# Mixture-of-experts results added to the output in DRAM by accumulating scatters, instead of read back and summed per tile of tokens

## The chip, the cores and the metric

The kernel runs on one core of a Trainium2 chip. The metric is device time in microseconds (us), the median of several executions. One execution of the kernel before was also recorded by the hardware profiler; all rows below are from it.

## The reference

One transformer block with modulation from a conditioning vector, all in float32:

```
x = L0_attn_x                                  # (4, 1024, 256)
sa, ca, ga, sb, cb, gb = silu(c) @ wmod        # per batch; |ga|, |gb| held above 0.25
h = layernorm(x) * (1 + ca) + sa
x = x + ga * attention(h)                      # 16 heads of 16, causal, with output projection
h = layernorm(x) * (1 + cb) + sb
x = x + gb * moe(h)
```

`moe(h)`: logits of 8 experts for each of the 4096 tokens, the two largest chosen, their softmax as weights; each expert is `silu(h @ w1[e]) @ w2[e]` with a hidden width of 512; a token's result is the weighted sum over its two experts. The reference computes all experts for all tokens; the kernel computes only the chosen pairs of token and expert.

## The kernel before

Attention runs first, batch by batch, in 16 groups of four heads. `schedule()` writes one list of steps, in order, for the whole kernel; each engine walks through it and issues its own part of each step, so the list sets the order on every engine and on both DMA-issuing queues (SP's and POOL's). Semaphore waits are between steps.

After attention of a batch, step `x2` stores the residual stream x of that batch to DRAM (tensor X2), steps `h2` normalise and modulate it in place, and `h2st` stores that to DRAM (H2D, rows of 256 numbers). Routing gives each of the 8192 pairs a place in a list sorted by expert, padded to whole tiles of 128 rows: NF = 71 tiles. Segment 0 (batches 0 to 2) fills tiles 0 to 40, segment 1 (batch 3, and what is left over) tiles 41 to 70. Steps `hot`, `tok` and `table` turn this round into three tables: TOK (the token's row for each row of a tile), ROW (where its result goes) and TE (the tile's expert).

Then 71 tiles go through the experts. In iteration t of the loop (line 281) the order is: `xload` t+3, `ystore` t-3, `up` t, `turnx` t+1, `turnh` t-1, `down` t-2.
- `xload` (L906, POOL queue): a gather by TOK of 128 rows of H2D into XL, three buffers; it waits for the transposes of tile t-3.
- `turnx` (L1666, L1667, L1031, L1443): TensorE transposes XL; ScalarE and VectorE split the result in a high and a low part.
- `up` (L1481, PH): 6 matrix products with the expert's w1; ScalarE applies SiLU (L1037). `turnh` (L1688, L1045, L1448): transposes and the same split.
- `down` (L1481, PY): 12 products with w2; VectorE copies PSUM to YO (L1455), four buffers.
- `ystore` (L912, POOL queue): a scatter by ROW of YO into the DRAM tensor YT, in which each token has a row for its first and one for its second expert. No two scatters write the same row, and none waits for another.

The last attention steps of batch 3 (`div`, `out`, `ln2`, `logits`, routing of segment 1) are interleaved with the first 40 tiles or so.

At the end each of the 32 tiles of 128 tokens is combined. `gat` (L785, L787, SP queue) loads its rows of X2 into XR and its two rows per token of YT into YG, after the scatters of all tiles that can hold them. `comb` weights the first result (L1051, ScalarE), adds the weighted second (L1460), multiplies by gb (L1464) and adds x (L1467, all VectorE). `out_st` (L792) stores the tile. The 24 tiles of segment 0's batches run beside experts' tiles 56 to 70; the 8 of batch 3 wait for the last scatter.

Of the kernel before, what the change touches and what calls it, by code (L numbers as in the profile page):

```python
# [17 lines left out]
NG = 4 * B  # L18
# [19 lines left out]
EMPTY = 128 * (NF - NA)  # L38

# [49 lines left out]
def schedule():  # L89
# [37 lines left out]

    def table(s, at, rest, late):
# [8 lines left out]
    def combine(n):  # L137
        return [(0, ("comb", n)), (0.5, ("out_st", n))]
# [43 lines left out]
    place(1, 12, one("gates"))  # L182
    place(0, -36, one("bvb"))
# [13 lines left out]
    place(NG - 1, 16, one("weights", 0))  # L197
# [83 lines left out]
    for t in range(NF + 12 + NT):  # L281
# [16 lines left out]
        while at and min(at) <= (t if t < NF + 11 + NT else max(at)):  # L298
# [14 lines left out]

LATE = ()

RING = 10


def gat_ring(n):

    return n % RING if n < 3 * NT else RING + n - 3 * NT
# [43 lines left out]
    "weights": {"wt": 3},  # L367
    "hot": {"hot": 1},
    "tok": {"px": 1, "tok": 1},
    "table": {"table": lambda s, n: 2 + s * (2, 1, 0, 0, 0)[n]},  # L370
# [6 lines left out]
    "xload": {"xl0": lambda t: 16 * (t % 3 == 0), "xl1": lambda t: 16 * (t % 3 == 1), "xl2": lambda t: 16 * (t % 3 == 2)},  # L377
    "turnx": {"fx": 1, "xhi": 1, "xlo": 1},
# [4 lines left out]
    "gat": {f"yg{i}": (lambda n, i=i: 32 * (gat_ring(n) == i)) for i in range(RING + NT)},  # L383
    "comb": {"cmb_a": 1, "comb": 2, "cmb_d": lambda n: int(n not in LATE), "cmb_p": lambda n: int(n in LATE)},
    "out_st": {f"o{i}": (lambda n, i=i: 16 * (gat_ring(n) == i)) for i in range(RING + NT)},
}

FIRST = {"c0": 16, "gbb": 16 * B, "wm0": 16, "wm1": 16, "ld_xa": 16, "ld_x0": 16, "ld_x1": 16, "ld_x2": 16, "ld_x3": 16, "ld_w": 16, "ld_bq": 16, "ld_o": 48, "ld_gw": 16,
# [30 lines left out]
def adaln_block(nc, x, wqkvT, b_qk, b_v, woT, b_o, gate_w, w1, w2, cT, wmod, iota, out):  # L419
# [8 lines left out]
    with ctx:  # L428
# [12 lines left out]
        TW = sb("TW", [128, 2, B * NT])  # L441
# [11 lines left out]
        TM1 = sb("TM1", [128, 2, NF])  # L453
        DU = sb("DU", [128, NF - NA])
# [70 lines left out]
        XL = sb("XL", [128, 3, D], F32, ffn)  # L525
        GB = sb("GB", [128, B, D], F32, ffn)
        end = ExitStack()
        YG = [sb(f"YG{i}", [128, 2, D], F32, end) for i in range(4)]
        XR = [sb(f"XR{i}", [128, D], F32, end) for i in range(4)]

        G3R = G3[:, :, :, :].rearrange("p b t n -> p (b t) n")
        YG += [XB[:, 3 * i:3 * i + 2, :] for i in range(2)] + [G3R[:, 3 * i:3 * i + 2, :] for i in range(4)]
        XR += [XB[:, 3 * i + 2, :] for i in range(2)] + [G3R[:, 3 * i + 2, :] for i in range(4)]
        end.close()
# [4 lines left out]

        last = ExitStack()  # L540
        YG += [sb(f"YGL{i}", [128, 2, D], F32, last) for i in range(NT)]
        XR += [sb(f"XRL{i}", [128, D], F32, last) for i in range(NT)]
        last.close()

# [19 lines left out]
        X2 = nc.dram_tensor("X2", [B, T, D], F32).ap()  # L564
        H2D = nc.dram_tensor("H2D", [B * T, D], F32).ap()

        YT = nc.dram_tensor("YT", [EMPTY + B * T * 2, D], F32).ap()
# [65 lines left out]
        def x2_tiles(b):  # L633
            return X2[b].rearrange("(t p) d -> p t d", p=128)

        def store_wait(lane, tiles):

            for t in range(tiles - 4, tiles):
                lane.wait_ge(*after(f"ys{t % 4}", "ystore", t))
# [4 lines left out]
        def sync_program(eng):  # L644
# [16 lines left out]
            for step in order:  # L661
# [75 lines left out]
                elif kind == "x2":  # L737
                    b = a[0]
                    sp.wait_ge(*after("om", "out", b, 3))
                    eng.dma_start(x2_tiles(b), xt(b * NT, (b + 1) * NT)).then_inc(S[f"x2{b}"].sem, 16)  # L740
                elif kind == "h2st":
# [3 lines left out]
                    eng.dma_start(H2D[b * T:(b + 1) * T, :].rearrange("(t p) d -> p t d", p=128),  # L745
# [22 lines left out]
                elif kind == "gat":  # L768
                    n = a[0]
                    b, r = n // NT, gat_ring(n)  # L770
                    if n == 0:
                        sp.wait_ge(*after("om", "out", B - 1, 3))
                        sp.wait_ge(*after("px", "tok", 1, 0))
                        for i in range(B):
                            eng.dma_start(GB[:, i, :].rearrange("p (k n) -> p k n", k=2),
                                          GD.rearrange("(t k b) n -> b t k n", k=2, b=B)[i, 3].partition_broadcast(128)
                                          ).then_inc(S["gbb"].sem, 16)
                        sp.wait_ge(S[f"h2s{B - 1}"], 16)
                        sp.wait_ge(*after("px", "lgt", B - 1, 3))
# [973 lines left out]
```

## Time and profile before

| | us |
|---|---|
| median of 3 runs | 1033.56 (1031.01 to 1035.2) |
| the profiled execution's own time | 1026.26 |
| its span | 1024.5 |
| TensorE busy | 910.5 (89% of the span) |
| VectorE busy | 738.2 (72%) |
| ScalarE busy | 577.4 (56%) |
| GpSimd busy (mostly issuing indirect DMAs in the last third) | 347.4 (34%) |

PE is TensorE's matmuls, PEld its weight loads, DVE VectorE, ACT ScalarE, POOL GpSimd, SP SyncE, which only issues DMAs. "L912" is line 912 of the kernel. A row of the timeline gives start and duration in us, engine, line, operation, and in brackets how long the engine had been idle and what ended that. The chain of waits is followed back from the last instruction of the execution.

### The profile page before, as it was taken

The numbers are of one execution on the slowest core, as the hardware profiler recorded it, in microseconds if no ns is written. First come the engines' busy times: TensorE is split into PE (matmuls) and PEld (weight loads), VectorE is DVE, ScalarE is ACT, GpSimd is POOL, SyncE is SP. The second block draws the span as 40 slices with busy tenths as digits, with TensorE's granted clock in tenths as the row PEclk, the third lists the DMA queues.
The fourth block names the chain that finished last, engine by engine and source line by source line (L and its number), as shares of the span: only waits on it lengthen the run. The fifth ranks groups of instructions, "written<-read, shape, count | busy, mean of one in ns | idle before, by whom it ended". The sixth has DMA issues, their size and how long they took to land.

```text
span 1024.5 us, 19379 instructions
## 1 busy us (share of the span) xinstructions
PE 910.5 (89%) x6174; PEld 535.3 (52%) x6174; DVE 738.2 (72%) x2346; ACT 577.4 (56%) x1257; POOL 347.4 (34%) x302
## 2 busy tenths in 40 slices
PE   5798899998899999989999888878699999999990
PEld 3443335333445334544443443423498899999880
DVE  8788766879666889757689767799337675444697
ACT  3235576676586667576666747557534534334452
POOL 1422021242424124325003433003177456655630
PEclk8899899999999999999999997989999999999995
DMA  8436436327316166253463565103413323222698
GB/s 275 123 63 125 62 77 140 62 39 145 66 27 138 41 101 139 66 74 89 73 117 100 124 112 170 36 23 111 137 47 124 99 68 104 78 78 68 207 297 293
DMA packets 83235, 110.61 MB, mean 108 GB/s; under 512 B 15930, under 2 KB 56434, under 8 KB 83138
## 3 DMA queue, kind: packets, MB, share of 16 engines
q1 hardware_dynamic: 75506, 89.45, 37.4%
q0 software_dynamic: 6816, 18.62, 5.8%
q10 hardware_dynamic: 816, 1.32, 0.4%
q8 instruction: 53, 0.87, 0.4%
q14 instruction: 44, 0.36, 0.1%
HBM read 69.42 MB, written 35.41 MB: 102 GB/s over the span
## 4 chain that ended last, share of the span: by engine, by line
PE 63%; DVE 14%; ACT 11%; issue 5%; POOL 3%; DMA 3%; SPq 1%; POOLq 0%; ACTq 0%; DVEq 0%
PE PO L1604 11%; PE PY L1481 9%; PE PS L1584 9%; PE PH L1481 9%; PE PM L1561 8%; ACT PR L979 5%; PE PHT L1688 3%; PE PX L1616 2%; PE PX L1530 2%; DVE MXF L1282 2%; PE PS L1588 2%; PE PX L1633 2%; DVE JK L1279 2%; PE PX L1539 1%; PE PX L1540 1%
## 5 line engine op out<-in xcount | busy, mean ns | idle before, releaser
L979 ACT ACTIVATE PR<-PS 128x512 f32<-128x512 f32 (+3 forms) x768 | 335.1, 497 | 165.0 <-PE PS L1588 128.4
L1279 DVE CUSTOM_DVE_ANT_0 JK<-PM,MK 128x128 bf16<-128x128 f32 (+3 forms) x512 | 239.6, 484 | 57.8 <-PE PM L1561 56.9
L1561 PE MATMUL PM<-QK 128*128 128x512 bf16 (+3 forms) x768 | 251.5, 336 | 26.9 <-DVE MXF L1282 15.6
L1584 PE MATMUL PS<-QK 128*128 128x512 bf16 (+3 forms) x768 | 250.7, 337 | 12.5 <-ACT PR L979 10.3
L1282 DVE TENSOR_REDUCE MXF<-PM 128x1 f32<-128x512 f32 x256 | 175.2, 684 | 76.5 <-PE PM L1561 74.8
L1584 PEld LDWEIGHTS PS<-QK 128*128 128x128 bf16 x768 | 75.2, 98 | 175.3 <-ACT PR L979 110.1
L1604 PE MATMUL PO<-PR,V 128*17 128x512 f32 (+3 forms) x1536 | 164.0, 500 | 0.0
L1561 PEld LDWEIGHTS PM<-QK 128*128 128x128 bf16 x768 | 76.0, 99 | 101.0 <-DVE MXF L1282 36.3
L1481 PE MATMUL PY<-W2S,HT 128*128 x852 | 120.2, 291 | 4.9 <-issue 4.3
L1037 ACT ACTIVATE HS<-PH 128x512 f32<-128x512 f32 x71 | 42.5, 598 | 135.4 <-PE PH L1481 133.3
L906 POOL DMA_INDIRECT XL<-H2D,TOK x71 | 78.7, 1109 | 113.6 <-DVE TE L1422 65.1
L1481 PE MATMUL PH<-W1S,XT 128*128 x426 | 112.5, 399 | 4.0 <-DVE XT L1443 3.5
L1588 PE MATMUL PS<-MT,identb 128*128 128x128 bf16 x512 | 112.5, 222 | 0.0
L1481 PEld LDWEIGHTS PY<-W2S,HT 128*128 128x128 f32 x852 | 107.2, 191 | 5.6 <-issue 5.5
L1443 DVE TENSOR_TENSOR XT<-PXT,XT 128x256 fp32r<-128x256 f32 x71 | 30.0, 422 | 106.6 <-ACT XT L1031 106.6
L847 POOL TENSOR_TENSOR SF<-SF,SP 128x512 f32<-128x512 f32 x28 | 32.4, 1157 | 215.2 <-ACT SP L969 215.1
L912 POOL DMA_INDIRECT YT<-YO,ROW x71 | 74.9, 1055 | 85.2 <-DVE YO L1455 76.1
L1481 PEld LDWEIGHTS PH<-W1S,XT 128*128 128x128 f32 x426 | 75.7, 189 | 18.3 <-issue 5.9
L1588 PEld LDWEIGHTS PS<-MT,identb 128*128 128x128 bf16 x512 | 50.8, 99 | 33.0 <-issue 6.3
L865 POOL TENSOR_TENSOR OP<-OP,LP 128x1024 f32<-128x1024 f32 x7 | 16.5, 2357 | 125.5 <-DMA LP<-LR 125.5
L1448 DVE TENSOR_TENSOR HT<-PHT,HT 128x512 fp32r<-128x512 f32 x71 | 49.0, 690 | 4.0
L1604 PEld LDWEIGHTS PO<-PR,V 128*17 128x17 f32 x1536 | 25.6, 96 | 34.4 <-issue 25.9
(263 smaller groups left out, 1201.6 us busy)
## 6 DMA issues: line engine op xcount, KB each, us to landing
QK<-SD SPq DMA_DIRECT2D x180, 128.0 KB
SD<-SP SPq DMA_DIRECT2D x42, 256.0 KB, 2.7
OP<-OS SPq DMA_DIRECT2D x64, 64.0 KB
LP<-LR SPq DMA_DIRECT2D x64, 64.0 KB, 2.3
W1S<-in_w SPq DMA_DIRECT2D x8, 512.0 KB, 5.8
W2S<-in_w SPq DMA_DIRECT2D x8, 512.0 KB, 4.8
X<-XA SPq DMA_DIRECT2D x3, 1024.0 KB, 9.1
H2D<-XA SPq DMA_DIRECT2D x3, 1024.0 KB, 4.9
```

Source lines behind the costliest of these rows:

```text
L906: eng.indirect_dma_start(XL[:, t % 3, :], None, H2D[0:(B if t >= NA else B - 1) * T, :], bass.IndirectOffsetOnAxis(ap=TOK[:, t:t + 1], axi ...
L912: eng.indirect_dma_start(YT, bass.IndirectOffsetOnAxis(ap=ROW[:, t:t + 1], axis=0), YO[:, t % 4, :], None, bounds_check=EMPTY - 1 + B * T ...
L979: eng.activation(PR[:, slot, i, c0:512], PS[m % 3][:, c0:512], ACT.Exp, scale=0.25).then_inc(S["exp"].sem, 1)
L1037: eng.activation(HS[:, t % 2, :], PH[t % 2][:, :], ACT.Silu).then_inc(S["silu"].sem, 1)
L1279: eng.tensor_tensor_reduce(JK[:, jk % 2, 0:w], PM[m % 3][:, 0:w], MK[:, 512 - w:512], 1.0, -3.0e38, ALU.add, ALU.max, MXA[:, mb, h, qt:qt ...
L1282: eng.tensor_reduce(MXF[:, mb, h, qt - 4:qt - 3], PM[m % 3][:, 0:w], AX.X, ALU.max).then_inc(S["mx"].sem, 1)
L1448: eng.tensor_tensor(HT[:, t % 2, 1, :, :], PHT[t % 2][:, :, :], HT[:, t % 2, 0, :, :].bitcast(F32), ALU.subtract).then_inc(S["hlo"].sem, 1)
L1481: last = eng.matmul(out_, stat[:, part, c, :], wt[:, bass.ds(v, 1), c, :].rearrange("p a n -> p (a n)"), start=(j == 0 and c == 0), stop=( ...
L1561: eng.matmul(PM[m % 3][:, 0:128 * (k1 - k0)], QK[:, r, h, 0, qt * 128:(qt + 1) * 128], QK[:, r, h, 1, k0 * 128:k1 * 128], start=True, stop ...
L1584: last = eng.matmul(PS[m % 3][:, c0:512], QK[:, r, h, 1, j * 128:(j + 1) * 128], QK[:, r, h, 0, 512 * f + c0:512 * f + 512], start=True, s ...
L1588: last = eng.matmul(PS[m % 3][:, c0:c0 + 128], identb[:, :], MT[:, :], start=False, stop=True, skip_group_check=True)
L1604: last = eng.matmul(PO[32 * i:32 * i + 17, c0:512], V[g // 4 % 2][:, j, 4 * (g % 4) + i, :], PR[:, (m - 1 + i // 2) % SLOTS, i % 2, c0:512 ...
```

## The change

- The output tensor in DRAM becomes 4096 + 128 rows; the first 4096 are returned. Step `x2` stores the residual x straight into its rows. The last 128 are filled once (with rows of x) and take the results of padding rows.
- `ystore` becomes an accumulating scatter (`compute_op=ALU.add`) to the token's row of the output. Since a token has two experts, a row can be hit by two tiles, so `ystore` t now waits until `ystore` t-1 has landed.
- The factors must be in the tile before it is stored. H2D's rows grow to 514 numbers: h, the row of gb of the token's batch (written by step `grow`, four DMAs on ACT's queue, DRAM to DRAM), and the token's two weights (step `wst`, SP queue, in pieces of 8 bytes). `xload` gathers all 514. A new DVE instruction in `turnx` picks the weight of this row's expert (WP), and the copy PSUM to YO becomes one instruction that multiplies by it and by gb.
- XL becomes a ring of six buffers that are held until YO is made: `xload` t waits for `down` t-6, not for the transposes of t-3.
- `gat`, `comb`, `out_st`, YT, X2 and the loads of gb (GB) are gone; the loop ends three iterations after the last tile.
- The tables are computed a little differently: ROW is the token, KK selects the weight.

```diff
-    place(45, one("weights", 1))
-    for n in range(3 * NT):
-        place(NL + 2.5 + 0.6 * n, one("gat", n))
-        place(NL + 4.5 + 0.6 * n, combine(n))
-    for n in range(3 * NT, B * NT):
-        place(NF + 2, one("gat", n))
-        place(NF + 8 + n - 3 * NT, combine(n))
+    place(24, weights(1))
...
-    for t in range(NF + 12 + NT):
+    for t in range(NF + 3):
...
+                elif kind == "wst":
+                    s = a[0]
+                    sl = slice(SEGS[s][0] * NT, SEGS[s][1] * NT)
+                    sp.wait_ge(*after("wt", "weights", s))
+                    eng.dma_start(H2D[:, 2 * D:WIDE].rearrange("(n p) k -> p n k", p=128)[:, sl, :],
+                                  TW[:, sl, :]).then_inc(S["ws"].sem, 16)
+            for i in range(4):
+                sp.wait_ge(S[f"ys{i}"], S[f"ys{i}"].n)
...
                 elif kind == "xload":
                     t = a[0]
-                    po.wait_ge(*after("table", "table", int(t >= NA), 4))
-                    for b in range(B if t >= NA else B - 1):
+                    s = segment(t)
+                    rows = SEGS[s][1] * T
+                    po.wait_ge(*after("table", "table", s, 4))
+                    for b in range(SEGS[s][1]):
                         po.wait_ge(S[f"h2s{b}"], 16)
-                    if t >= 3:
-                        po.wait_ge(*after("fx", "turnx", t - 3))
+                    po.wait_ge(S["gr"], 16 * B)
+                    po.wait_ge(*after("ws", "wst", s))
+                    if t >= XS:
+                        po.wait_ge(*after("yo", "down", t - XS))
...
                 elif kind == "ystore":
                     t = a[0]
+                    s = segment(t)
+                    rows = B * T + 128 if s else SEGS[0][1] * T
                     po.wait_ge(*after("yo", "down", t))
+                    for b in range(SEGS[s][1]):
+                        po.wait_ge(S[f"x2{b}"], 16)
+                    if s:
+                        po.wait_ge(S["dz"], 16)
+                    if t:
+                        po.wait_ge(*after(f"ys{(t - 1) % 4}", "ystore", t - 1))
                     eng.indirect_dma_start(
-                        YT, bass.IndirectOffsetOnAxis(ap=ROW[:, t:t + 1], axis=0), YO[:, t % 4, :], None,
-                        bounds_check=EMPTY - 1 + B * T * 2, oob_is_err=True).then_inc(S[f"ys{t % 4}"].sem, 16)
+                        out[0:rows, :], bass.IndirectOffsetOnAxis(ap=ROW[:, t:t + 1], axis=0), YO[:, t % 4, :], None,
+                        bounds_check=rows - 1, oob_is_err=True, compute_op=ALU.add).then_inc(S[f"ys{t % 4}"].sem, 16)
...
+                elif kind == "grow":
+                    b = a[0]
+                    ac.wait_ge(*after("gd", "gates"))
+                    eng.dma_start(H2D[b * T:(b + 1) * T, D:2 * D].rearrange("r (k n) -> r k n", k=2),
+                                  GD.rearrange("(t k b) n -> b t k n", k=2, b=B)[b, 3].partition_broadcast(T)
+                                  ).then_inc(S["gr"].sem, 16)
...
                 elif kind == "turnx":
                     t = a[0]
+                    dv.wait_ge(*after("table", "table", segment(t), 4))
+                    dv.wait_ge(*after(f"xl{t % XS}", "xload", t))
+                    if t >= XS:
+                        dv.wait_ge(*after("yo", "down", t - XS))
+                    eng.tensor_tensor_reduce(WJ[:, t % XS, :], XLS[t % XS][:, 2 * D:WIDE], KK[:, t, :], 1.0, 0.0, ALU.mult, ALU.add,
+                                             WP[:, t % XS:t % XS + 1]).then_inc(S["wp"].sem, 1)
...
                     if t >= 4:
                         dv.wait_ge(*after(f"ys{t % 4}", "ystore", t - 4))
-                    eng.tensor_copy(YO[:, t % 4, :], PY[t % 2][:, 0:256]).then_inc(S["yo"].sem, 1)
+                    dv.wait_ge(*after("wp", "turnx", t))
+                    eng.scalar_tensor_tensor(out=YO[:, t % 4, :], in0=PY[t % 2][:, 0:D], scalar=WP[:, t % XS:t % XS + 1],
+                                             in1=XLS[t % XS][:, D:2 * D], op0=ALU.mult, op1=ALU.mult).then_inc(S["yo"].sem, 1)
```

## Rows read from the trace of the kernel before

**Rows 1.** The page: span, and the chain of waits by engine.
```profile
span 1024.5 us, 19379 instructions
PE 63%; DVE 14%; ACT 11%; issue 5%; POOL 3%; DMA 3%; SPq 1%; POOLq 0%; ACTq 0%; DVEq 0%
```

**Rows 2.** Windows: start:end, length, busy us of each engine, PEclk, DMA share, GB/s.
```profile
741.00:820.00 79.00, 76.49 (x531) 69.15 (x531) 43.57 (x128) 36.05 (x73) 51.98 (x46) 1.00 0.28 88
823.00:945.00 122.00, 122.00 (x857) 111.14 (x856) 65.70 (x165) 47.75 (x105) 71.64 (x68) 1.00 0.26 81
985.00:1000.00 15.00, 14.01 (x97) 12.30 (x95) 13.93 (x34) 7.69 (x17) 4.93 (x5) 1.00 0.91 290
```

**Rows 3.** Timeline: first YO, tile 19's and 20's, the last three.
```profile
740.53 0.43 DVE L1455 COPY YO<-PY 128x256 f32<-128x256 f32 x1 [3.14 <-PE PY L1481]
...
822.74 0.42 DVE L1455 COPY YO<-PY 128x256 f32<-128x256 f32 x1
823.98 1.03 POOL L912 DMA_INDIRECT YT<-YO,ROW  x1 [1.33 <-DVE YO L1455]
825.31 1.04 POOL L906 DMA_INDIRECT XL<-H2D,TOK  x1 [0.30 <-issue]
826.22 0.42 DVE L1455 COPY YO<-PY 128x256 f32<-128x256 f32 x1
827.45 1.03 POOL L912 DMA_INDIRECT YT<-YO,ROW  x1 [1.10 <-DVE YO L1455]
...
995.52 0.41 DVE L1455 COPY YO<-PY 128x256 f32<-128x256 f32 x1
...
997.77 0.42 DVE L1455 COPY YO<-PY 128x256 f32<-128x256 f32 x1
...
1000.72 0.42 DVE L1455 COPY YO<-PY 128x256 f32<-128x256 f32 x1
```

**Rows 4.** The scatter's line L912, issue to landing, 900 to 950 us.
```profile
L912 POOL DMA_INDIRECT YT<-YO,ROW x14: 1029/1031/1039, 900.9 to 947.9; - x14
DMA to landing us min/median/max: 2.5/2.5/2.5
```

**Rows 5.** The same line, 985 to 1004 us, beside the loads of the combine.
```profile
L912 POOL DMA_INDIRECT YT<-YO,ROW x6: 982/983/996, 985.9 to 1001.9; - x6
DMA to landing us min/median/max: 3.6/4.4/5.2
```

**Rows 6.** Chain of waits, order of time, after the last tile: start, us, what.
```profile
1000.72 0.43 DVE YO L1455
...
1001.20 0.49 issue
1001.70 0.22 POOLq L428
1001.92 4.54 DMA YT<-YO,ROW
...
1006.55 4.55 DMA YGL<-YT
...
1011.13 0.52 ACT YGL L1051
...
1021.84 0.42 DVE XRL L1467
```

**Rows 7.** DMA view, 823 to 945 us: POOL's queue, packets, MB, share of 16 engines.
```profile
q0 software_dynamic: 3312, 9.05, 23.4%
XL<-H2D,TOK POOLq DMA_INDIRECT x34
YT<-YO,ROW POOLq DMA_INDIRECT x34, 2.5
```

**Rows 8.** DMA view, whole span: queue, count, KB each, us to landing.
```profile
LP<-LR SPq DMA_DIRECT2D x64, 64.0 KB, 2.3
LP<-LD SPq DMA_DIRECT2D x8, 32.0 KB, 1.7
LR<-LP SPq DMA_DIRECT2D x8, 32.0 KB, 1.5
X<-XA SPq DMA_DIRECT2D x3, 1024.0 KB, 9.1
```

**Rows 9.** Timeline of DVE, one tile's interval beside two combines.
```profile
965.70 0.42 DVE L1455 COPY YO<-PY 128x256 f32<-128x256 f32 x1
966.04 0.48 DVE L1460 SCALAR_TENSOR_TENSOR YG<-YG,TW 128x256 f32<-128x256 f32 x1
966.55 0.43 DVE L1464 TENSOR_TENSOR YG<-YG,GB 128x256 f32<-128x256 f32 x1
...
969.60 0.41 DVE L1455 COPY YO<-PY 128x256 f32<-128x256 f32 x1
```

**Rows 10.** ACT's queue: one DMA issue, ns min/median/max.
```profile
L926 ACTq DMA_DIRECT2D W<-in_wqkvT x1: 521/521/521, 1.9 to 1.9; - x1
```

**Rows 11.** Windows around the loads of the next group's QK.
```profile
268.00:286.00 18.00, 15.98 (x122) 9.98 (x120) 8.70 (x28) 12.09 (x28) 9.68 (x8) 1.00 0.68 100
286.00:300.00 14.00, 13.22 (x82) 5.50 (x81) 9.31 (x29) 12.01 (x26) 1.16 (x1) 1.00 0.05 9
```

More of the change, by code:

```diff
@@ L126, in route, with weights @@
         return [(0 if n % many else rest, ("route", s, n)) for n in range(NR)]
+    def weights(s):
+        return [(0, ("weights", s)), (0, ("wst", s))]
     def table(s, at, rest, late):
@@ L182, in schedule @@
     place(1, 12, one("gates"))
+    for b in range(B):
+        place(3 + b, 2, one("grow", b))
     place(0, -36, one("bvb"))
@@ L196, in schedule @@
     place(NG - 2, 0, route(0, 0.5))
-    place(NG - 1, 16, one("weights", 0))
+    place(NG - 2, 6, weights(0))
     for k, parts in table(0, 6, 0.5, 2):
@@ L297, in schedule @@
             order.append(("down", t - 2))
-        while at and min(at) <= (t if t < NF + 11 + NT else max(at)):
+        while at and min(at) <= (t if t < NF + 2 else max(at)):
             now[0] = min(at)
@@ L367 @@
     "weights": {"wt": 3},
+    "wst": {"ws": 16},
+    "grow": {"gr": 16},
     "hot": {"hot": 1},
     "tok": {"px": 1, "tok": 1},
-    "table": {"table": lambda s, n: 2 + s * (2, 1, 0, 0, 0)[n]},
+    "table": {"table": lambda s, n: (2 + 2 * s, 2 + s, 2, 2, 3)[n]},
     "h2st": {f"h2s{i}": (lambda b, i=i: 16 * (b == i)) for i in range(B)},
@@ L376 @@
     "low": {"sp_d": lambda e: 1 + int(e == 2)},
-    "xload": {"xl0": lambda t: 16 * (t % 3 == 0), "xl1": lambda t: 16 * (t % 3 == 1), "xl2": lambda t: 16 * (t % 3 == 2)},
-    "turnx": {"fx": 1, "xhi": 1, "xlo": 1},
+    "xload": {f"xl{i}": (lambda t, i=i: 16 * (t % XS == i)) for i in range(XS)},
+    "turnx": {"fx": 1, "wp": 1, "xhi": 1, "xlo": 1},
     "up": {"fh": 1, "silu": 1},
@@ L524, in adaln_block @@
         sb("PAD1", [128, D], F32, ffn)
-        XL = sb("XL", [128, 3, D], F32, ffn)
-        GB = sb("GB", [128, B, D], F32, ffn)
+        XL = sb("XL", [128, 2, WIDE], F32, ffn)
+        XLS = [XL[:, i, :] for i in range(2)]
+        G3R = G3[:, :, :, :].rearrange("p b t n -> p (b t n)")
+        XLS += [G3R[:, WIDE * i:WIDE * (i + 1)] for i in range(XS - 2)]
         end = ExitStack()
[L528 to L534, printed above, removed]
         HOTS.append([sb("OLO1", [128, 1, PAIRS[1], 128], BF16, end), sb("OHI1", [128, 1, PAIRS[1], NF - NA], BF16, end),
@@ L538, in adaln_block @@
         ffn.close()
[L540 to L543, printed above, removed]
         PX = ps("PX", [128, 512])
@@ L633, in x2_tiles, with segment @@
         def x2_tiles(b):
[L634 to L639, printed above, removed]
+            return out[b * T:(b + 1) * T, :].rearrange("(t p) d -> p t d", p=128)
+        def segment(t):
+            return int(t >= NA)
         def od_wait(lane, g):
@@ L794, in sync_program @@
-            for i in range(RING + NT):
-                sp.wait_ge(S[f"o{i}"], S[f"o{i}"].n)
+                elif kind == "wst":
[6 more added lines that the diff above has]
+                sp.wait_ge(S[f"ys{i}"], S[f"ys{i}"].n)
@@ L1660, in tensor_program @@
                     t = a[0]
-                    pe.wait_ge(*after(f"xl{t % 3}", "xload", t))
+                    pe.wait_ge(*after(f"xl{t % XS}", "xload", t))
                     if t >= 1:
```

144 lines of the change are left out of this document (43 added, 101 removed).

## The prediction, made before the changed kernel was run

> **What bounds the kernel now.** I read the page first [rows 1]: TensorE carries 63% of the chain that ended last, DMA only 3%. The change touches the last third, so the next view is the windows over the experts' tiles. From 823 to 945 us TensorE is busy for 122.00 of 122 us at a granted clock of 1.00, while VectorE has 65.70 and POOL 71.64 [rows 2]. There nothing but TensorE sets the pace, and the period is the distance of two copies to YO: 826.22 - 822.74 = 3.48 us; over many tiles 3.47, which I use [rows 3]. Between 741 and 820 us steps of batch 3's attention take TensorE too and tiles come every 5.2 us at times: from the first copy (740.53) to tile 19's (822.74) 19 periods take 82.2 us, 4.33 each [rows 3]. From tile 19 to tile 70 (1000.72) 51 periods take 178.0 us, 3.49 each. Last, the chain of waits behind the last tile [rows 6]: copy at 1000.72, scatter issued at 1001.92, landed after 4.54 us, then a load of 4.55 us, then ScalarE and eight combines on VectorE up to 1022.3, then the last store up to the end at 1024.5. That is 1024.5 - 1001.1 = 23.4 us without any matmul. This tail is what the change can win; the scatters themselves are hidden now, since none waits for another.
>
> **What the change removes.** In the tail only the last scatter is left. It was slow (4.54 us; 3.6 to 5.2 beside the loads of the combine, DMA share 0.91) [rows 2, 5, 6]; in quiet stretches it takes 2.5 from issue to landing [rows 4]. With 0.78 us from the end of the copy (1001.14) to the start of POOL's instruction (1001.92) [rows 3, 6], the tail shrinks to 0.8 + 2.5 = 3.3 us if the add costs nothing: 20.1 won. The combines that run beside tiles 56 to 70 go as well. One interval with two of them on VectorE is 969.60 - 965.70 = 3.90 instead of 3.47 [rows 9]; five intervals in that stretch are so, 5 x 0.43 = 2.2 us. But the last two tiles come 2.3 and 3.0 us after the ones before them (995.52, 997.77, 1000.72) [rows 3], closer than scatters in line can follow (below), which takes about 1.5 back. Sum of what can be won: 20.1 + 2.2 - 1.5 = about 21 us.
>
> **What it adds: scatters in line.** `ystore` t waits for the landing of `ystore` t-1. POOL needs 0.78 us from a release to the start of an indirect DMA (823.16, the end of the copy, to 823.98 is 0.82; the last is 0.78) [rows 3, 6], and that counts in each link, because the wait is the last to end. So scatters can't follow each other faster than P = L + 0.78, with L from issue to landing. For the plain scatter P = 2.5 + 0.78 = 3.28 us [rows 4], against 3.47 that TensorE gives: the chain is hidden, by 0.19 us. So the whole forecast hangs on what the add does to L. Queued behind the waiting instruction on POOL is the gather `xload` of t+4; when it is held, XL comes late, TensorE waits, and the tiles take P as well; the four YO buffers only soften that.
>
> Below what L is this free? Up to P = 3.47 (L = 2.69) nothing is lost. Above that I follow it: with the chain the bound, slack in the slow first 19 tiles absorbs it (4.33 mean against P), and tile 19's scatter starts at 823.16 + 0.78 + 1.04 + 0.30 = 825.3, behind the gather that is now released by the same copy [rows 3]. Then 51 links and one landing: end of span = 825.3 + 51 x (L + 0.78) + L = 865.1 + 52 L. It equals 1024.5 at L = 3.07. Half a microsecond in L decides the sign, and each 0.1 us above costs 5.2 us (more beyond P = 4.33, where the first tiles are held too: by a small recurrence over all 71 copies, +57 us at L = 4.0).
>
> The trace shows no accumulating DMA, so L is bounded. Below: 2.5, the plain scatter [rows 4]. It can't be shorter, as the same bytes are still sent to the same kind of place. Above: the add as a load of its own ahead of the write; the nearest load is LP<-LR, 64 KB, 2.3 us [rows 8], so 4.8. Between them: a scatter's or gather's share of the 16 DMA engines is 0.234 x 122 / 68 = 0.42 us [rows 7]; the add must read 128 KB more, so its data part about doubles: +0.42. A read of DRAM must come back before the write: a 32 KB load takes 1.7 against 1.5 for a store of the same size [rows 8]: +0.2. POOL's 1.03 us [rows 4] is descriptor writing for 128 rows; a third address for each row would be up to half more, +0.5, or nothing if that time is fixed: I take +0.2. L = 2.5 + 0.42 + 0.2 + 0.2 = 3.3 us, P = 4.1, both nearer to the plain scatter's row than to the other bound. End of span 865.1 + 52 x 3.3 = 1036.7: +12.2 us.
>
> The Trainium skill, "Collectives: The Full Stack", section "The bandwidth ceiling: the fold count and why AG ≠ RS ≠ AR", says that the add in the DMA engine costs no cycles of its own, and that it is the second read that halves the rate. By that rule only the doubled data part counts, L = 2.9, and the span would end at 1015.9, 8.6 us early; no row here shows an add, so the trace neither bears it out nor speaks against it. It is the third case below. Its page "DMA: Bandwidth & Descriptors", section "Rules for kernel authors", adds that another write to the same bytes that lands during an accumulate is lost, so the wait between scatters can't be left out here.
>
> **Other edits.** The copy to YO becomes a multiply with a second operand: 0.48 instead of 0.42 [rows 9], and a small instruction on 2 columns is added, at most 0.2. VectorE then has some 0.3 us more per tile at 65.70/122 = 54% busy [rows 2]: hidden by TensorE; if that cover went it would be 71 x 0.3 = 21 us. The gather carries 257 KB instead of 128 and is released 2 us later, but TensorE wants it two periods later, 6.9 us, and by the scatter's row and the doubled data it lands in 2.5 + 0.42, some 3 us: nothing. The four `grow` DMAs are issued by ScalarE during attention, 0.52 us each [rows 10], and carry 4 MB from DRAM to DRAM. They fall on the loads of the next group's QK, when the DMA engines are full for 14 us (share 0.68 over 18 us, then 0.05) [rows 11]; a store of 1 MB lands in 9.1 [rows 8], so these loads could end 9 us late where they have about 10 to spare. I take +1 us for the four, bounds 0 and +8. `wst` is off every path: segment 0's weights stand in the order a whole group of attention before the first gather, and segment 1's at iteration 24, fourteen before tile 41 is gathered. The tables have about as many small instructions as before, and lie beside a TensorE that is never idle there [rows 2]: 0. The store of x into the output has the bytes of the old one: 0.
>
> **Sum.** +12.2 + 1 = +13 us on the profiled execution's span; its own time goes from 1026.3 to 1039.5. The runs have a median of 1033.56, 7.3 above the profiled one; the same +13 gives 1047.
>
> **The cases.**
> - Chain of scatters is the bound, L of 3.1 or more (chance 0.6). For it: the margin of 0.19 us is smaller than any of the three additions. Own range: L from 3.1 to 4.0, +2 to +57: 1036 to 1091; value 1047.
> - The chain stays hidden, L up to about 2.75 (chance 0.15). For it: 16 engines hold eight rows each, and reads of one row may run beside writes of another, so that only a small part of the extra read shows. Then the tail's 21 us are won, less 1: 1014.
> - Chain longer than TensorE's period but shorter than break-even, L of 2.75 to 3.0, what the second read alone gives (chance 0.2). 865.1 + 52 x 2.9 = 1015.9, 8.6 early, less 1: 1026 on the runs.
> - The scatters are free, but QK's loads come late four times by `grow` (chance 0.05): 4 x 2 = +8 against -21: 1021. Against it: waits for QK's loads don't show in the chain now.
> The mechanism on the other side is thus one: whether L stays below 3.07 us.
>
> That the change doesn't do what it says can be ruled out for the tail: no step reads back.
>
> **Chances.** A difference of under 0.5% (5 us) is no change by what can be measured here. Faster by more: 0.33 (cases two and four and most of three); within: 0.09 (L of 2.97 to 3.17); slower: 0.58. The range of 8 in 10 goes from 1015, which leaves part of the hidden chain out, to 1088 (L = 4.0).
>
> **What would show it.** Right: L912 shows landings of 3.3 us and is released by its own DMA in most of its 71 instances, its starts 4.1 us apart after 823; TensorE busy some 85% of that stretch, PE PXT waiting for the gather; no matmul-free tail beyond the last scatters. Wrong: starts still 3.47 apart and TensorE at 100% (hidden, the tail won); or landings above 4.0 (then it costs 60 us and more); or idle before PM<-QK about groups 5 to 8.

## The result, and the profile after

| | us |
|---|---|
| changed kernel, median of 4 runs | 1136.46 (1130.28 to 1146.09) |
| before, on the same chip, median of 4 runs | 1034.38 (1031.01 to 1037.2) |
| ratio, with its 95% interval | 1.0997 [1.0912, 1.1082] |
| span of the profiled execution | 1135.7 (before 1024.5, [rows 1]) |

The change makes the kernel 10% slower. The forecast was +13 us, and the range ended at 1088: the direction was right, the size far off. The two profiled spans differ by 111.2 us, and the place of the first copy to YO splits them: 740.53 before [rows 3] and 785.95 now. So 45.4 us come before the first expert's tile is finished, and 65.8 us behind it.

The page of the kernel after: span, the chain of waits by engine, and the same chain by line.

```profile
span 1135.7 us, 19288 instructions
PE 35%; DMA 26%; DVE 10%; issue 9%; ACT 8%; SPq 6%; POOL 5%; POOLq 0%; another core or an unknown queue 0%; ACTq 0%; DVEq 0%
DMA out<-YO,ROW 20%; PE PO L1560 9%; PE PS L1540 7%; PE PM L1517 6%; SPq L658 4%; ACT PR L948 3%; PE PX L1486 2%; DVE MXF L1245 2%; DVE JK L1242 2%; PE PX L1572 2%; PE PS L1544 1%; DMA LD<-OS 1%; PE PX L1495 1%; PE PX L1496 1%; ACT SF L931 1%
```

TensorE carried 63% of the chain before [rows 1]; now it is 35%, and DMA went from 3 to 26, of which the accumulating scatter has 20. SPq, which is SP's queue itself, went from 1 to 6; 4 of these are L658, the loads of QK.

First the scatters. The scatter's line in the kernel after: durations in ns, min/median/max, and who releases it, in us and times.

```profile
L881 POOL DMA_INDIRECT out<-YO,ROW x71: 1552/1589/3625, 788.5 to 1129.3; - x71
its engine sat idle before it (us, times) until:
  DMA out<-YO,ROW: 85.8, 45
```

The same scatter in the DMA view: KB are not given, the last number is the median us from issue to landing.

```profile
out<-YO,ROW POOLq DMA_INDIRECT x71, 3.8
```

One such instruction on POOL takes 1.59 us where the plain scatter took 1.03, and it lands after 3.8 us where that one took 2.5 [rows 4]. In 45 of 71 cases POOL sits idle until the scatter before has landed. The chain of waits at the end (start, us, what) shows the links themselves:

```profile
1110.65 3.84 DMA out<-YO,ROW
...
1115.33 3.82 DMA out<-YO,ROW
1119.14 0.02 issue
1119.16 0.02 POOLq L399
1119.18 0.04 issue
1119.23 0.03 POOLq L881
1119.26 0.72 issue
1119.98 3.84 DMA out<-YO,ROW
...
1124.65 3.78 DMA out<-YO,ROW
```

Landing at 1119.14, next start at 1119.98: 0.84 us. A link, from the start of one scatter to the start of the next, is 3.8 + 0.85 = 4.65 us, against the 3.47 us in which TensorE makes a tile. What TensorE makes of it is in the windows (start:end, length, busy us of each engine, PEclk, DMA share, GB/s):

```profile
823.00:945.00 122.00, 99.48 (x683) 86.58 (x684) 70.80 (x255) 46.49 (x90) 68.36 (x50) 0.99 0.50 97
```

It was busy for all of these 122 us before [rows 2]; now for 99.48. It waits for gathers, as the waits of 740 to 1136 us say (engine and line, what it waited for: us in total, times, longest). The ring of six buffers appears there under two names, XL and G:

```profile
PE PXT L1622 <- DMA G<-H2D,TOK: 36.1, 29, 3.1
PE PXT L1622 <- DMA XL<-H2D,TOK: 16.3, 13, 2.8
```

The gathers are late because they stand on POOL behind a scatter that waits for its predecessor.

The tail that the change was to win is nearly as long as before: 21.1 us from the last copy to YO (1114.57) to the end, against 23.8. The copies run ahead of the chain, and the scatters left over follow one another there.

Now the part ahead of 786 us. `grow` in the DMA view, with its landing time, and SP's queue in the timeline (start, us, what):

```profile
H2D<-GD ACTq DMA_DIRECT2D x4, 1024.0 KB, 23.4
```

```profile
197.82 23.25 SPq L658 DMA_DIRECT2D QK<-SD  x12
```

Twelve issues of loads of QK took SP's queue 23.25 us, beside a `grow` issued at 200 us. The twelve issues at the same place in the kernel before:

```profile
197.78 6.15 SPq L685 DMA_DIRECT2D QK<-SD  x12
```

Twelve take 25.51 and 17.30 us beside the second and the fourth `grow`. The third was issued at 311.14, when the loads of its group were already out (302.00 to 307.57); beside it four other loads take 13.80. Each group of attention begins its loads with one QK<-ZR, and the distances between these show what each `grow` cost. Before they start at 196.97, 234.11, 272.27, 317.26 and 354.74, now at 197.00, 246.48, 301.19, 347.74 and 399.54: 12.3, 16.6, 1.6 and 14.3 us more, 44.8 of the 45.4. The one `grow` that met no load of QK cost next to nothing.

In the windows from 200 to 420 us (columns as above), first after, then before, TensorE loses 34 us and its granted clock is 0.90 instead of 1.00:

```profile
200.00:420.00 220.00, 171.08 (x1113) 74.78 (x1135) 131.82 (x443) 120.16 (x267) 48.72 (x39) 0.90 0.46 88
```

```profile
200.00:420.00 220.00, 205.33 (x1436) 92.78 (x1433) 174.01 (x620) 151.18 (x339) 67.01 (x54) 1.00 0.47 91
```

The DMA share is the same over these 220 us, 0.46 and 0.47, and nearly so the bytes, 88 and 91 GB/s. So a want of bandwidth doesn't explain it; `b_growx` below confirms this with engines that are fully busy.

### The profile page after: what moved, and what is told of

The parts are those of the page before. It is cut to its first block, busy times and chain, and to the rows that moved or that the text cites. A ratio compares the mean times of both kernels' runs of the same rounds, so it can differ in the third digit from the quotient of the medians.

```text
span 1135.7 us, 19288 instructions
## 1 busy us (share of the span) xinstructions
PE 925.3 (81%) x6098; PEld 538.4 (47%) x6174; DVE 715.3 (63%) x2394; ACT 572.9 (50%) x1225; POOL 389.0 (34%) x302
## 4 chain that ended last, share of the span: by engine, by line
PE 35%; DMA 26%; DVE 10%; issue 9%; ACT 8%; SPq 6%; POOL 5%; POOLq 0%; another core or an unknown queue 0%; ACTq 0%; DVEq 0%
DMA out<-YO,ROW 20%; PE PO L1560 9%; PE PS L1540 7%; PE PM L1517 6%; SPq L658 4%; ACT PR L948 3%; PE PX L1486 2%; DVE MXF L1245 2%; DVE JK L1242 2%; PE PX L1572 2%; PE PS L1544 1%; DMA LD<-OS 1%; PE PX L1495 1%; PE PX L1496 1%; ACT SF L931 1%
## 5 line engine op out<-in xcount | busy, mean ns | idle before, releaser
L1517 PE MATMUL PM<-QK 128*128 128x512 bf16 (+3 forms) x727 | 238.7, 336 | 62.3 <-DVE MXF L1245 42.5
L1540 PE MATMUL PS<-QK 128*128 128x512 bf16 (+3 forms) x733 | 240.5, 339 | 15.5 <-ACT PR L948 11.1
L1560 PE MATMUL PO<-PR,V 128*17 128x512 f32 (+3 forms) x1536 | 168.8, 513 | 0.1
L881 POOL DMA_INDIRECT out<-YO,ROW x71 | 115.4, 1625 | 125.3 <-DMA out<-YO,ROW 85.8
L866 POOL DMA_INDIRECT XL<-H2D,TOK x24 | 26.6, 1109 | 105.1 <-DVE ROW L1380 67.8
L866 POOL DMA_INDIRECT G<-H2D,TOK x47 | 53.3, 1134 | 13.7 <-issue 13.6
## 6 DMA issues: line engine op xcount, KB each, us to landing
H2D<-GD ACTq DMA_DIRECT2D x4, 1024.0 KB, 23.4
```

The lines of the kernel that those rows point to most:

```text
L866: eng.indirect_dma_start(XLS[t % XS], None, H2D[0:rows, :], bass.IndirectOffsetOnAxis(ap=TOK[:, t:t + 1], axis=0), bounds_check=rows - 1, ...
L881: eng.indirect_dma_start(out[0:rows, :], bass.IndirectOffsetOnAxis(ap=ROW[:, t:t + 1], axis=0), YO[:, t % 4, :], None, bounds_check=rows - ...
L1517: eng.matmul(PM[m % 3][:, 0:128 * (k1 - k0)], QK[:, r, h, 0, qt * 128:(qt + 1) * 128], QK[:, r, h, 1, k0 * 128:k1 * 128], start=True, stop ...
L1540: last = eng.matmul(PS[m % 3][:, c0:512], QK[:, r, h, 1, j * 128:(j + 1) * 128], QK[:, r, h, 0, 512 * f + c0:512 * f + 512], start=True, s ...
L1560: last = eng.matmul(PO[32 * i:32 * i + 17, c0:512], V[g // 4 % 2][:, j, 4 * (g % 4) + i, :], PR[:, (m - 1 + i // 2) % SLOTS, i % 2, c0:512 ...
```

## The experiments

Ratios are to the kernel before, run beside each on its chip. The first time given behind "Measured" is the median of the runs; positions ("first copy to YO") and spans are those of the profiled execution.

### Each half of the change alone, in the kernel before

`b_grow` adds only the four DMAs, into a scratch tensor that nobody reads:

```diff
+        place(3 + b, 2, one("grow", b))
...
+                    eng.dma_start(GROW[b * T:(b + 1) * T, D:2 * D].rearrange("r (k n) -> r k n", k=2),
+                                  GD.rearrange("(t k b) n -> b t k n", k=2, b=B)[b, 3].partition_broadcast(T)
```

> The kernel before, with nothing added but the four grow DMAs (4 MB, DRAM to DRAM, pieces of 512 bytes, on ACT's queue) into an unused DRAM tensor, at the same steps as in the changed kernel. Theory (grow alone delays attention by blocking the QK loads on SP's queue): first copy to YO near 786 us instead of 740.5, time near 1079 (+45). Rival (the delay of attention in the changed kernel comes of something else, or grow's 4 MB is hidden as predicted): within 8 us of before.

Measured: 1067.85 us, ratio 1.0391 [1.0322, 1.046], span 1067.6; first copy to YO at 783.66, 43.1 later than before. The DMAs land after 22.7 us. Nearly the whole early loss, 43.1 of 45.4 us, is there, with nothing else of the change.

`b_wait` adds only the wait from scatter to scatter, the scatters staying plain:

```diff
+                    if t:
+                        po.wait_ge(*after(f"ys{(t - 1) % 4}", "ystore", t - 1))
```

> The kernel before, with each plain scatter waiting for the landing of the one before it, and nothing else. Theory (a link costs L + 0.85 us, with L = 2.5 for the plain scatter it fits in the 3.47 us period): +0 to +6 us, all of it near the tail, where the scatter takes 3.5 to 4.4 us beside the combine's loads. Rival (waiting in line is itself the main cost, whatever the scatter does): +30 us or more.

Measured: 1043.58 us, ratio 1.015 [1.0099, 1.0202]: 15 us slower, more than the 0 to 6 expected, and far from the rival's 30. In the quiet stretch most links are 3.34 us, as forecast. Beside the loads of the combine (tiles 56 to 70), where landings took 3.6 to 5.2 us [rows 5], links are 3.3 to 6.6; the last copy to YO comes 11.8 us later than before. A chain has to be priced in its busiest stretch, not only in its quiet one. In the changed kernel these loads are gone.

### What in `grow` costs 45 us

`a_fix` is the changed kernel in which a `grow` loads the row once into all partitions of SBUF (128 KB) and stores from there, with pieces of 1 KB, at later steps of the group:

```diff
-                    eng.dma_start(H2D[b * T:(b + 1) * T, D:2 * D].rearrange("r (k n) -> r k n", k=2),
-                                  GD...[b, 3].partition_broadcast(T))
+                    eng.dma_start(GX.rearrange("p (k n) -> p k n", k=2), GD...[b, 3].partition_broadcast(128))
+                elif kind == "gput":
+                    eng.dma_start(H2D[b * T:(b + 1) * T, D:2 * D].rearrange("(t p) d -> p t d", p=128),
+                                  GX.unsqueeze(1).broadcast_to([128, NT, D]))
```

> The changed kernel, with grow sent another way: gb's row is first loaded to 128 partitions of SBUF (128 KB) and from there stored to H2D in pieces of 1 KB, at steps 12 and 15 of the same windows. Same result. Theory (form and place of grow cost 45 us): first copy to YO back near 741, time near 1090. Rival (any 4 MB more in attention costs that): stays above 1115.

Measured: 1089.09 us, ratio 1.0585 [1.0525, 1.0645]; first copy to YO at 736.17, links still 4.65. The early loss is gone and nothing else is: 61 us remain, and with the 40 of `b_grow` that makes 101, against the 102 of the change.

`a_late` leaves `grow` as it was and issues it seven positions later in the attention group:

```diff
-        place(3 + b, 2, one("grow", b))
+        place(3 + b, 9, one("grow", b))
```

> The changed kernel, with the four grow DMAs in their old form but at step 9 of the same windows instead of step 2, behind the QK loads instead of beside them. If the cost is the collision with the QK loads: near 1092, 45 us less than the changed kernel. If the 24 us that each DMA holds the DMA engines cost whatever comes: still above 1120. Between: other DMAs of the window (the rows of maxima, the stores of SD) wait behind it.

Measured: 1117.11 us, ratio 1.087 [1.0793, 1.0948]; first copy at 764.13, landing 20.9 us. By the profile the place halves the loss but doesn't remove it. Most of what stays comes from another load. The group with the second `grow` (issued at 243.16) takes 15.2 us more than before, and there a load of 32 KB, the sums of the softmax, lands late. It lands after 1.7 us in the kernel before [rows 8]. Its line from 240 to 260 us in `a_late`, who waited for it, and its landing:

```profile
L701 SPq DMA_DIRECT2D LP<-LD x1: 341/341/341, 247.9 to 247.9; - x1
  DVE LP L1277: 16.4, 1
DMA to landing us min/median/max: 16.8/16.8/16.8
```

`b_growx` takes `b_grow` and lets the DMAs, of the same size, at the same steps and from DRAM to DRAM, read a row of its own for each row that they write:

```diff
-                                  GD.rearrange("(t k b) n -> b t k n", k=2, b=B)[b, 3].partition_broadcast(T)
+                                  x[b].rearrange("r (k n) -> r k n", k=2)
```

> The kernel before plus four DMAs as in grow (1 MB each, DRAM to DRAM, pieces of 512 bytes, same steps, same queue), but with x's rows as the source, so that each piece is read from its own address instead of all 2048 from the same 1 KB. If the piece and the way (DRAM to DRAM) make the 23 us: landing near 23 us, time +40. If it is the re-reading of one row: landing below 12 us, time within 15 us of before.

Measured: 1024.98 us, ratio 0.9992 [0.996, 1.0023]; landing 9.4 us. The DMA view of `b_grow`, and then that of `b_growx`:

```profile
GROW<-GD ACTq DMA_DIRECT2D x4, 1024.0 KB, 22.7
```

```profile
GROW<-in_x ACTq DMA_DIRECT2D x4, 1024.0 KB, 9.4
```

Neither the 4 MB nor DRAM on both sides costs anything measurable. The windows of `b_growx` show the first of the four at work: the DMA engines are busy all the time, and TensorE hardly idles.

```profile
195.00:205.00 10.00, 9.72 (x81) 4.48 (x84) 8.65 (x30) 7.14 (x19) 0.00 (x0) 1.00 1.00 224
```

But the edit changed two things and not one. The queue of ACT on the pages of `b_grow` and of `b_growx`:

```profile
q10 hardware_dynamic: 9072, 5.51, 3.5%
```

```profile
q10 hardware_dynamic: 4976, 5.51, 2.0%
```

The same bytes take 4096 packets less. So the four DMAs moved in pieces of 512 bytes with gb's row as source, in pieces of 1 KB with x's rows, although the text above says 512 for both. Both the address that is read again and again and the number of pieces, 2048 against 1024 per DMA, can be the cause. The kernel before has DMAs that copy rows of GD into SBUF, in pieces of 512 bytes too:

```profile
G<-GD SPq DMA_DIRECT2D x4, 384.0 KB, 6.1
GB<-GD SPq DMA_DIRECT2D x4, 128.0 KB, 3.5
```

The four G<-GD, issued one behind the other from 141.4 us, write 3072 such pieces, each of twelve rows read 128 times, and land within 9 us. So neither pieces of 512 bytes nor 128 readings of a row are slow in themselves when they go to SBUF. What remains is one row read 2048 times, or 2048 small pieces from DRAM to DRAM, or both together; no run here separates them.

In `b_grow` TensorE waits 9.1 us for one load of QK between 200 and 420 us, and 28.2 us more are put down to VectorE's maxima (MXF); in `b_growx` no wait for QK shows there, and 4.5 us for MXF.

### What in the scatters costs 61 us

`a_fix_plain` is `a_fix` with plain scatters in the same chain, so the tokens' sums are left out:

```diff
-                        bounds_check=rows - 1, oob_is_err=True, compute_op=ALU.add)
+                        bounds_check=rows - 1, oob_is_err=True)
```

> The changed kernel with grow sent by way of SBUF, its scatters in line but plain: they overwrite the rows instead of adding, so sums are left out. Theory (the add makes L 3.8 instead of 2.5): landings 2.5, links 3.3 to 3.4, below the period of 3.47, span near 1007 plus what grow still costs, some 85 us below the same kernel with the add. Rival (waiting in line or the wider gather is the cost): span above 1060.

`a_fix_rows` is `a_fix` with accumulating scatters, but each to a block of 128 rows of its own, one of 16 blocks in turn, and without waits; the sums are left out too:

```diff
-                    if t:
-                        po.wait_ge(*after(f"ys{(t - 1) % 4}", "ystore", t - 1))
...
-                            eng.tensor_copy(ROW[:, ts], TK[:, 0, ts]).then_inc(tb.sem, 1)
+                            eng.scalar_tensor_tensor(out=ROW[:, t0:t1], in0=IO[:, 0:t1 - t0], scalar=128.0,
+                                                     in1=PI[:, 0:1].broadcast_to([128, t1 - t0]), op0=ALU.mult,
+                                                     op1=ALU.add).then_inc(tb.sem, 1)
```

> The changed kernel with grow by way of SBUF, accumulating scatters that wait for none: each tile adds to rows of its own among 16 places, in contiguous rows, so the tokens' sums are left out. Theory (the add only costs where the next scatter waits for it): tiles every 3.5 us, L912's successor still 1.6 us on POOL and landing in 3.8 or a little more, span near 1010. Rival (adds are slow in throughput: the DMA engines or POOL can't do one each 3.47 us): tiles above 4 us apart, span above 1050.

Measured: 1015.18 us, ratio 0.9821 [0.9715, 0.9927], and 1008.66 us, ratio 0.9758 [0.97, 0.9816]. The scatter's line from 880 to 980 us in `a_fix`, `a_fix_plain` and `a_fix_rows`, one fence each:

```profile
L884 POOL DMA_INDIRECT out<-YO,ROW x21: 1589/1589/1590, 882.9 to 975.9; - x21
  DMA out<-YO,ROW: 28.8, 17
DMA to landing us min/median/max: 3.7/3.8/3.9
```

```profile
L884 POOL DMA_INDIRECT out<-YO,ROW x28: 1029/1030/1042, 879.3 to 979.7; - x28
  DMA out<-YO,ROW: 6.2, 6
```

```profile
L882 POOL DMA_INDIRECT out<-YO,ROW x30: 1591/1591/1593, 879.0 to 979.7; - x30
```

In these 100 us the three kernels start 21, 28 and 30 scatters; the kernel before starts 29. The chain alone is hidden (links of 3.30 between slower ones), the add alone is hidden (1.59 us on POOL, tiles 3.47 apart for the most part). From first to last copy to YO the two take 261.9 and 262.4 us, the kernel before 260.2 and `a_fix` 329.9. Only both together cost: the add makes L 3.8, the chain puts all of L on the path. That `a_fix_rows` writes contiguous rows doesn't explain its speed: `z` below adds to the tokens' scattered rows without waits, its scatters land after 3.9 us in the median, and its tiles too come 3.47 apart up to the first sum. Between the chained add and the chained plain scatter lie 7.6% of the time, some 79 us, by the ratios (about 66 to 91 with their intervals; `a_fix_plain` has only two runs), and 70 us by the profiled spans, 1087.5 and 1017.5.

`a_fix_64` is `a_fix` with scatters of the tile's first 64 rows only; the others' results are left out:

```diff
-                        out[0:rows, :], bass.IndirectOffsetOnAxis(ap=ROW[:, t:t + 1], axis=0), YO[:, t % 4, :], None,
+                        out[0:rows, :], bass.IndirectOffsetOnAxis(ap=ROW[0:64, t:t + 1], axis=0), YO[0:64, t % 4, :], None,
```

> The changed kernel with grow by way of SBUF; each accumulating scatter stores only 64 of a tile's 128 rows, so half the results are left out. It divides the 1.3 us that the add puts on L into a part by rows and a fixed part. If POOL's 1.59 us is by rows: about 0.8 to 1.3, and landing 0.3 us less after it. If fixed: 1.59 and 3.8 stay. Expected from POOL by rows for the added part only (0.56 us): about 1.0 to 1.3 us on POOL, L near 3.1, span near 1040.

Measured: 1043.22 us, ratio 1.0096 [1.0064, 1.0129]. The same line and stretch:

```profile
L884 POOL DMA_INDIRECT out<-YO,ROW x25: 1439/1439/1457, 882.3 to 979.2; - x25
```

The time came out as expected (span 1039.2), the 1.0 to 1.3 us on POOL did not. Half the rows take only 0.15 us off POOL's 1.59. If that is linear, no more than 0.3 us of the 1.59 goes by rows, so of the 0.56 that the add puts on POOL at least 0.26 is fixed; how much more isn't shown, since no plain scatter of 64 rows was run. The link falls by 0.68 us, from 4.65 to 3.97, so 0.53 us of it lie outside POOL's instruction.

### Is there a version that wins?

The chain is there because two tiles can hit one row. `z` takes that reason away: based on `a_fix`, the second expert's results go to a second, zero-filled half of a larger output tensor, no scatter waits for another, and at the end of a batch one accumulating DMA of 1 MB adds the second half to the first. The padding rows go to four blocks in turn.

```diff
-                    if t:
-                        po.wait_ge(*after(f"ys{(t - 1) % 4}", "ystore", t - 1))
...
+                elif kind == "sum":
...
+                    first, second = [out[r:r + T, :].rearrange("(p t) d -> p (t d)", p=128) for r in (b * T, SECOND + b * T)]
+                    eng.dma_start(first, second, accum_op=ALU.add, max_dma_last_dim=8192)
```

> Full result, built from what the runs showed: grow by way of SBUF; accumulating scatters that wait for none, since a token's first result is added to its row of the output (which holds x) and its second to a row of a second half, filled with zeros during attention; tiles' padding rows go to four blocks in turn. After the last scatter one accumulating DMA per batch adds the second half to the output, 1 MB each, three of them beside the last tiles. Expected: tiles at 3.5 us as in the run without waits, last scatter near 1000 us, then 3.8 + 0.9 + a 1 MB accumulate of 5 to 9 us: span 1011 to 1016, about 13 us below before (ratio near 0.985). Rival: the accumulates of the first three batches, on POOL's queue, hold up its gathers, or the 4 MB of zeros delay attention: span above 1025.

Measured: 1026.75 us, ratio 0.9998 [0.9974, 1.0022], span 1020.6: no gain on the kernel before, a miss by some 5 us. The last copy to YO comes at 1004.64 where `a_fix_rows` had 997.93. A gather issued 1.8 us behind a sum (984.34 and 986.12) landed late, and TensorE waited; the gather's line from 980 to 1000 us in `z`:

```profile
L878 POOL DMA_INDIRECT G<-H2D,TOK x2: 1071/1104/1137, 981.9 to 986.1; - x2
  PE PXT L1666: 2.6, 1
DMA to landing us min/median/max: 4.5/6.9/9.2
```

`z2` was to cut the sums into pieces of 256 KB:

```diff
-        place(NL + 4 + 3 * b, one("sum", b))
+        for q in range(4):
+            place(NL + 4 + 8 * b + 2 * q, one("sum", b, q, 4))
```

> The version z with its sums in smaller pieces: each of the three early batches' sums is four DMAs of 256 KB, one every second tile from tile 45 on, where z issued 1 MB at once at three places; the last batch's sum is two DMAs of 512 KB where z had one. Theory (a gather queued behind a 1 MB accumulate lands late, 9.2 us in z, and holds TensorE): a gather now waits behind a quarter of it, so lands in at most 5 us, within the ring's slack; the last copy to YO comes at 998 to 1001 instead of 1004.6, and the span is 1013 to 1017 instead of 1020.6; on the runs 3 to 8 us faster than before. Rival (it is POOL's issuing time, or the DMA share as such, not the size of one transfer): twelve issues of about 1 us on POOL in place of three of 1.5 add work there and the bytes are the same, so the last copy stays at 1004 or later and the time stays equal to before's.

Measured: 1031.05 us, ratio 1.0041 [1.0017, 1.0064], span 1032.0: slower by 0.4%. That is a slip in the schedule and no verdict on the theory: NL is 56, so the twelve places run from iteration 60 to 82, and only 71 tiles are there. The line of the sums from 1010 us on shows five early pieces and the two of the last batch behind the last tile:

```profile
L904 POOL DMA_DIRECT2D out<-out x7: 790/1347/2212, 1014.2 to 1017.9; - x7
DMA to landing us min/median/max: 5.3/9.1/11.3
```

`z3` has six pieces of 512 KB, all inside the loop, and one sum for the last batch:

```diff
-        for q in range(4):
-            place(NL + 4 + 8 * b + 2 * q, one("sum", b, q, 4))
+        for q in range(2):
+            place((60, 62, 64, 66, 68, 69)[2 * b + q], one("sum", b, q, 2))
```

> As z, with the early batches' sums as six DMAs of 512 KB, issued in iterations 60, 62, 64, 66, 68 and 69 (z2 had twelve places from 60 to 82, seven of which thus fell behind the last tile, which was not meant), and the last batch's sum as one DMA again. Theory (what held z was a gather that landed behind 1 MB; z2's loss was only its seven sums behind the last tile): a gather behind 512 KB lands in 5 to 7 us, inside the ring's slack; tiles stay 3.47 apart to the end, and from the first to the last copy to YO it takes 262 to 264 us (z 266.8, z2 264.5); the tail is z's 16 us; span 1014 to 1020, 0 to 6 us faster than before on the runs. Rival (the add's own traffic is too dense there whatever its pieces, or the bound is now elsewhere): copies 266 us or more from first to last, or a tail over 18 us, and no gain on before.

Measured: 1023.1 us against 1031.44 of before on that chip, ratio 0.9906 [0.9871, 0.994]: about 1% faster than the kernel before, and the fastest whole version here. The reasons held only in part. From first to last copy it takes 264.65 us, better than `z` (266.8) but not the 262 to 264 expected, and TensorE still waits for gathers there; the line of the gathers from 960 to 1000 us in `z3`:

```profile
L879 POOL DMA_INDIRECT G<-H2D,TOK x6: 1069/1110/1154, 962.4 to 989.4; - x6
  PE PXT L1668: 1.8, 2
```

Its profiled span, 1021.3, is no shorter than `z`'s 1020.6; the gain stands on the ratios of the repeated runs (6 of `z3`, 12 of `z`, on different chips). How much of it is due to the smaller pieces is therefore not settled. Behind the last scatter's landing (1010.93) the last sum still takes up to 1021.3, 10.4 us.

A wait for the scatter before the last one (t-2 instead of t-1) would give links of (3.8 + 0.85)/2 = 2.3 us by the numbers above. It wasn't tried: two neighbouring tiles can share a row of the output, so it would not be free of races.

## Why the prediction was wrong, point by point

- **What bounds the kernel, and the form of the loss: right.** The chain of scatters became the bound; L881 is released by its own DMA in 45 of 71 cases, TensorE sits at 82% of the stretch from 823 to 945 (99.48 of 122; "some 85%" was forecast), PE PXT waits for the gather, no tail without matmuls beyond the last scatters. That it came out slower is no luck of the unforeseen `grow` either: `a_fix`, without that loss, is still 61 us slower. But even `a_fix`, at 1094 by its ratio, lies above the 1088 at which the range ended: the chain alone was already priced too low.
- **"P = 2.5 + 0.78 = 3.28" for a plain chain: right** (3.30 in `a_fix_plain`), and hidden there. In `b_wait`, beside the combine's loads, it is not (15 us).
- **The term L = 3.3: mis-sized, 3.8 measured.** Of its parts, "+0.2" for the third address on POOL is the worst: POOL's instruction grew by 0.56 us. The bounds given there were 0 and 0.5, argued from descriptors per row, and both the value and the argument failed: with 64 rows it is 1.44 us. The other two parts together were 0.62; if POOL's 0.56 counts fully in L, 1.3 - 0.56 = 0.74 is left for them. With L = 3.8 the formula of the prediction gives 865.1 + 52 x 3.8 = 1062.7, +38 us instead of +12. An estimate from `a_fix_64`: half the rows shorten the link by 0.68 us, so some 1.4 of its 4.65 us go by rows and the rest is fixed. What the Trainium skill, "Collectives: The Full Stack", section "The bandwidth ceiling: the fold count and why AG ≠ RS ≠ AR", says of the second read had given the prediction its other estimate, L = 2.9; here the trace doesn't agree, as the add costs 1.3 us and not one more data part of 0.42.
- **The formula: too short where P is above 4.33,** as the text said. With every link from the first on at 4.66, the scatters end at 741.8 + 70 x 4.66 + 3.8 = 1071.8, +47.3. Measured behind the first copy is +65.8. The rest, 18.5 us: the 70 links take 340.7 us and not 326.2 (14.5). Five of them, 5.57 to 5.86 us, stand beside the last attention steps, where POOL has a 1.6 us scatter, a 1.1 us gather and 3.1 us of its own adds per tile and is itself the bound (5.6 of the 14.5); six single ones of 5.7 to 6.6 make the other 8.8, and what held these isn't shown. The first scatter starts 2.58 us behind its copy (1.3 more), and the last one needs 6.4 us to the end instead of 3.8 (2.6). Beside the attention steps `a_fix_plain` has links of 5.25 and `a_fix_rows`, without a chain, 5.85: there POOL's added 0.56 us counts by itself, a cost that the prediction had nowhere.
- **"I take +1 us for the four" `grow`, bounds 0 and +8: wrong, +45.4.** This is the step that failed most. The prediction priced them as a store of 1 MB by the row of 9.1 us [rows 8]. `b_growx` has about that, 9.4 us landing, and no cost; `grow` landed in 23.4. The row had the right bytes, but each address was read once and the pieces were larger. The trace of before held nearer rows that the prediction didn't use: GB<-GD above copies the same rows of GD in the same pieces, 128 KB in 3.5 us, and G<-GD 384 KB in 6.1. Scaled to 1 MB by bytes they give estimates of 28 and 16 us, on both sides of the 23.4 measured. They aren't a sure price, since four of each ran at once and together moved 512 KB in some 5 us and 1.5 MB in 9, but they allowed an upper bound far above 9.1. The text also has the DMA engines full for 14 us there; its own window gives 0.68 x 18 = 12. And the case "QK's loads come late" was priced at 2 us each with a chance of 0.05; they came late three times and cost 12.3, 16.6 and 14.3 us, since SP's queue was held in issuing them, a thing that no row of before showed.
- **The tail, "about 21 us" won: right in sum on the runs, not in its parts.** `a_fix_plain` is 18.4 us under the kernel before beside it (1033.57 - 1015.18; 8 to 29 with its interval), `a_fix_rows` 24.9. But in the profiles the tail behind the last copy falls from 23.8 to 12.5 and 7.9 us, not to 3.3. Behind the last copy of `a_fix_plain` scatters still follow in line, 3.3 us apart, and some 2 us pass between the last landing and the end. Nor did the missing combines win 2.2 us: from first to last copy it takes 261.9 and 262.4 us, not less than the 260.2 before.
- **Multiply instead of copy, wider gather, `wst`, tables: 0, right.** In `a_fix_rows`, which has all of them, tiles come 3.47 apart in the quiet stretch.
- **The case "hidden", 1014 on the runs:** the add without the chain gives about that (1008.66). The forecast lacked the thought that the chain, not the add, is what a variant could drop.

The measured split is +45.4 (`grow`) + 65.8 (chain at 4.65 with its long links, less the 2.6 us by which the tail is shorter) = +111.2 on the span. It is a division of the span at one point, not an independent check; that is `b_grow` and `a_fix`, 40 + 61 = 101 of 102 us on the runs.

## What to carry to other kernels

A chain of dependent DMAs costs issue to landing plus the wake-up of the issuing engine, each time; when its margin under the bound is smaller (0.19 us here) than what is unknown of the new DMA, measure that one DMA first, or remove the dependency instead. A DMA that spreads one short row of DRAM over a megabyte in small pieces isn't priced by its bytes: look for a row of the trace with the same source and the same pieces, or go by way of SBUF, which took the whole loss away here. Where the work of one engine goes up by half a microsecond per tile, add up that engine's work in every stage, above all where other steps are interleaved.

## What the runs showed of the hardware

- An accumulating scatter of 128 rows of 1 KB: 1.59 us on POOL and 3.8 to landing, against 1.03 and 2.5 plain; with 64 rows 1.44 on POOL. A chain of them has links of 4.65 us, a plain one of 3.30.
- One 1 KB row of DRAM read by 2048 pieces of 512 bytes and written to DRAM: 22.7 us for 1 MB. Rows of their own in pieces of 1 KB: 9.4. A store from SBUF with pieces of 1 KB: 5.4. Whether the first is slow by its one address or by its pieces isn't separated.
- Beside such a DMA twelve issues on SP's queue took 23.25 us instead of 6.15, and a load of 32 KB landed after 16.8 us instead of 1.7.
- TensorE's granted clock was 0.90 in the mean from 200 to 420 us (1.00 is 2.4 GHz, the lower level 1.2), where it sat idle for these loads, and 1.00 before the change.
- An accumulating DMA of 1 MB from DRAM to DRAM took 7.8 to 10.4 us to land, and a gather of 257 KB issued behind one 9.2 us (3.5 in the median of all gathers of `z`).
